# A mixture-of-experts kernel: the routers' token-valued tile table written by VectorE token by token

## The reference, cut to what matters

```python
logits = flat @ router_w.T
probs = softmax(logits)
topk_prob, topk_idx = top_k(probs, 2)
topk_prob = topk_prob / sum(topk_prob)
for e in range(8):
    w_e = sum(topk_prob * (topk_idx == e))
    y = (silu(flat @ gate_w[e].T) * (flat @ up_w[e].T)) @ down_w[e].T
    out = out + w_e * y
```

## Time and profile before

| | |
|---|---|
| median of 3 runs | 1080.37 us (1078.08 to 1084.45) |
| profiled execution | 1077.55 us, its span 1075.7 us |
| TensorE busy | 917.6 us of the span |
| VectorE busy | 609.9 us |
| ScalarE busy | 551.9 us |
| first tail, line 527's first start to line 541's start | 120.27 to 138.84 us |
| second tail, the same | 810.12 to 828.67 us |
| mean granted TensorE clock | 0.898 |

### The profile page before, as it was taken

How to read it: one execution, slowest core, us unless ns; L and a number is a source line. 1 busy time by engine, 2 the same in 40 slices (tenths; PEclk the granted TensorE clock), 3 DMA queues, 4 the chain that set the end, 5 groups by cost and what they waited for, 6 DMA issues and landing times. The chain is left out here.

```text
span 1075.7 us, 20700 instructions
## 1 busy us (share of the span) xinstructions
PE 917.6 (85%) x6102; PEld 785.6 (73%) x6102; DVE 609.9 (57%) x1702; ACT 551.9 (51%) x1372; POOL 271.2 (25%) x274
## 2 busy tenths in 40 slices
PE   5656569999999999997378999998746899998998
PEld 3544458888888888886256777776625899997998
DVE  6887942332323323222777778767768555555786
ACT  6346543443434434343355555554436566667774
POOL 0000031121211212110763220000001544443775
PEclk9858569999999999999589999998655899999999
DMA  9655211111111111111843221102241344444654
GB/s 385 271 193 198 81 40 55 54 55 54 50 54 55 55 54 50 55 44 66 270 128 98 60 79 60 40 21 79 79 157 42 116 138 139 137 133 131 182 163 148
DMA packets 62231, 114.79 MB, mean 107 GB/s; under 512 B 9586, under 2 KB 43012, under 8 KB 60996
## 3 DMA queue, kind: packets, MB, share of 16 engines
q1 hardware_dynamic: 48900, 77.77, 20.5%
q0 software_dynamic: 12960, 35.41, 11.6%
q10 hardware_dynamic: 288, 0.47, 0.1%
HBM read 74.01 MB, written 39.59 MB: 106 GB/s over the span
## 5 line engine op out<-in xcount | busy, mean ns | idle before, releaser
L600 POOL DMA_INDIRECT experts_rows_sb<-h_rows,choices x142 | 137.5, 969 | 651.9 <-POOLq L428 325.9
L799 DVE TENSOR_TENSOR experts_a_sb<-experts_a_sb,experts_bankU 128x512 f32<-128x512 f32 x71 | 48.9, 689 | 223.1 <-PE experts_bankU L184 223.1
L747 ACT ACTIVATE experts_a_sb<-experts_bankG 128x512 f32<-128x512 f32 (+1 forms) x142 | 69.7, 491 | 90.4 <-PE experts_bankG L184 90.3
L760 ACT ACTIVATE experts_y_sb<-experts_bankY 128x256 f32<-128x256 f32 x142 | 54.7, 385 | 86.1 <-PE experts_bankY L181 66.6
L738 ACT ACTIVATE experts_hT<-experts_bankH 128x256 fp32r<-128x256 f32 x142 | 54.2, 382 | 80.5 <-PE experts_bankH L663 80.4
L1198 POOL DMA_INDIRECT attn_y<-y_rows,choices x64 | 65.6, 1024 | 108.3 <-DVE x_res L1652 55.9
L182 PE MATMUL experts_bankY<-down_high,experts_aT 128*128 x284 | 91.5, 322 | 0.3 <-DVE experts_aT L187 0.3
L183 PE MATMUL experts_bankY<-down_low,experts_aT 128*128 x284 | 79.8, 281 | 0.0
L184 PE MATMUL experts_bankY<-down_high,experts_aT 128*128 x284 | 79.8, 281 | 0.0
L923 POOL DMA_INDIRECT shared_y<-y_rows,choices x64 | 67.9, 1061 | 37.8 <-POOLq L555 18.5
L181 PE MATMUL experts_bankY<-down_plain,experts_aT_plain 128*128 x284 | 72.9, 379 | 0.0
(11 more groups left out here) (367 smaller groups left out, 2626.4 us busy)
## 6 DMA issues: line engine op xcount, KB each, us to landing
y_rows<-experts_y_sb SPq DMA_DIRECT2D x142, 128.0 KB, 1.9
h_rows<-xn SPq DMA_DIRECT2D x32, 256.0 KB, 2.2
mix_xT<-in_xt SPq DMA_DIRECT2D x4, 1024.0 KB, 12.0
x_res<-in_x SPq DMA_DIRECT2D x4, 1024.0 KB, 13.9
gate_raw<-in_L_ffn_gate_w SPq DMA_DIRECT2D x2, 2048.0 KB, 13.6
up_raw<-in_L_ffn_up_w SPq DMA_DIRECT2D x1, 4096.0 KB, 25.1
x_rows<-x_res SPq DMA_DIRECT2D x16, 256.0 KB
x_res<-x_rows SPq DMA_DIRECT2D x8, 512.0 KB, 4.7
```

Of the source, the lines that this page charges most:

```text
L600: nc.gpsimd.indirect_dma_start(rows[t % DEPTH][:, :], None, h_dram, bass.IndirectOffsetOnAxis(ap=ids_i[:, t:t + 1], axis=0)).then_inc(s_ro ...
L747: nc.scalar.activation(a_sb[i % RING][:, :], bankG[i % RING][:, 0:hidden], ACT.Silu if gate is not None else ACT.Relu).then_inc(s["act"], 1)
L799: nc.vector.tensor_tensor(a_sb[i % RING][:, :], a_sb[i % RING][:, :], bankU[i % RING][:, 0:hidden], ALU.mult).then_inc(s["a"], 1)
```

## The change

The tile table is written by VectorE with four instructions of 128x72 per batch, one for each tile of tokens. Each has two scalars per partition from memory: it compares the ramp with the token's `slot_tile` (`is_equal`) and multiplies the result by the token's number (`mult`). ScalarE's multiplication and the semaphore between VectorE and ScalarE are left out; the row table's instruction now signals `one_hot` itself. Both tails use the function, so both change.

```diff
-                s_equal, s_one_hot, s_spread = ([sem(f"{tag}_{n}{k}") for k in range(2)] for n in ("equal", "one_hot", "spread"))
+                s_one_hot, s_spread = ([sem(f"{tag}_{n}{k}") for k in range(2)] for n in ("one_hot", "spread"))
...
                     nc.scalar.activation(share[:, :], apart[:, :], ACT.Exp).then_inc(s["exp"], 1)
-                    for n in range(TILES // BATCH):
-                        for k in range(2):
-                            act.wait_ge(s_equal[k], n + 1)
-                            for i in range(BATCH):
-                                part = at_tile[k][n % RING][:, i * TABLE_T:(i + 1) * TABLE_T]
-                                last = nc.scalar.activation(part, part.bitcast(F32), ACT.Copy, scale=token[:, n * BATCH + i:n * BATCH + i + 1])
-                            last.then_inc(s_one_hot[k], 1)
...
                             if n >= RING:
                                 dve.wait_ge(s_spread[k], n - RING + 1)
-                            nc.vector.tensor_tensor(table(at_tile[k][n % RING]), K("ramp")[:, 0:TABLE_T].unsqueeze(1).broadcast_to([P, BATCH, TABLE_T]),
-                                                    tokens(slot_tile, at_j, TABLE_T), ALU.is_equal)
+                            for i in range(BATCH):
+                                nc.vector.tensor_scalar(at_tile[k][n % RING][:, i * TABLE_T:(i + 1) * TABLE_T], K("ramp")[:, 0:TABLE_T],
+                                                        slot_tile[:, at_j + i:at_j + i + 1], token[:, n * BATCH + i:n * BATCH + i + 1],
+                                                        ALU.is_equal, ALU.mult)
                             nc.vector.tensor_tensor(table(at_row[k][n % RING]), K("ramp").unsqueeze(1).broadcast_to([P, BATCH, P]),
-                                                    tokens(slot_row, at_j, P), ALU.is_equal).then_inc(s_equal[k], 1)
+                                                    tokens(slot_row, at_j, P), ALU.is_equal).then_inc(s_one_hot[k], 1)
```

## The result

The changed kernel takes 1092.7 us (median of 4 runs, 1091.91 to 1093.48), the kernel before 1079.22 (median of 4, 1077.1 to 1084.45). The ratio is 1.0111, with a 95% interval of 1.0084 to 1.0137, which is 9.1 to 14.8 us of 1079.22. So it is slower, by 13.5 us between the medians; the forecast's step from before to after, 15.2 us, lies 0.4 us above the upper end of that interval. The profiled execution took 1092.98 us (span 1091.1), 15.43 more than the profiled one of before.

The account below looks back on a forecast made before the run. The router tails lie on the path, VectorE and ScalarE level there. Per tail, 16 x (0.93 - 0.37) = 9.0 us less 1.30 gives 7.6 within rounding; two add 15.2 to 1080.37: 1095.6, likeliest 1095.5, range 1087 to 1106.

Parts of the forecast that it names:

- The bound: Both router tails: nothing of the expert stage runs beside them, so a change in their length shifts all behind.
- The spacing of the new instruction: VectorE's 128x72 instruction with two scalars from memory: 0.232 us from start to start, 0.93 for four.
- ScalarE's lag: End of each tail: ScalarE's last scaling ends after VectorE's last comparison; removing the scalings saves 1.30 us a tail.
- The small chain: VectorE's 1.40 us of work behind the batches: stays hidden by about 0.3 us under the 1.65 until the ids' read.
- The sum: A tail of 64 spacings plus 11.33 us: 26.2 us, 7.6 more than 18.57; two tails +15.2.
- The time: Whole kernel: likeliest 1095.5 us, from the median before of 1080.37 and the two tails' added time.
- The clock: TensorE's granted clock: 0.50 in the tails; its later rise may move by 3 us, 1.5 us a tail, range only.
- TensorE's wait between batches: In the tails, TensorE waits for VectorE about 0.65 us between batches.
- A: Rival: scalars read beside the instruction before, spacing 0.11 us, a tail of 18.4 us, kernel 1080.0; chance 0.10.
- B: Rival: new instruction starts when the last ends, spacing 0.316 us, kernel 1106.4; chance 0.15 together with spacing unshrunk by size.

Follow-up runs that it names:

- e4: The change in the second tail only, the first tail as in the kernel before: 1085.63 us, ratio 1.0059 to the kernel before.
- e1: The changed kernel with two constants in place of both scalars from memory in the four 128x72 instructions: 1081.97 us.
- e2: The kernel before with the tile table compared by four 128x72 instructions with one scalar from memory, ScalarE's scaling kept: 1086.72 us.
- e3: The changed kernel with each of the four small instructions 128 columns wide instead of 72: 1097.9 us.
- e6: The kernel before with both tables in float16 and their operands laid out in pairs, ScalarE scaling as before: 1078.0 us.
- e9: The changed kernel with float16 tables and the row table's operands in pairs: 1083.82 us.

## Why the prediction was right

- *The bound.* Right: the tails' length lies on the path, and all that follows shifts by it. From the read of the ids to TensorE's restart it is 7.29 us before and 7.28 after, and e4's tails add.
- *The spacing of the new instruction.* 0.232 forecast, 0.228 measured; the duration 0.316 and 0.311. It came from a row of another size with the same operands, corrected by a slope from rows with constants. e1, e2 and e3 show each term: 0.07 for the instruction, 0.06 per scalar from memory, 0.5 ns per element. The forecast batch was 1.53, measured 1.51.
- *ScalarE's lag.* Right: 1.30 us go from the end, and from the last row comparison's end (144.23) to the read (145.88) it is 1.65 us, as assumed. The small chain (lines 528 to 534 now) ends at 145.56 and stays hidden.
- *The sum.* 26.2 us a tail forecast, 25.9 measured; +15.2 forecast, +14.7 in the tails, +15.43 between the two profiled executions, +13.5 between the medians, with an interval of 9.1 to 14.8 that leaves out the 15.2 and holds the 14.7. So the tails' step was forecast 0.5 us too large, mostly by the spacing (64 x 0.004 us a tail).
- *The time.* 1095.5 forecast, 1092.7 measured. 1.2 of the 2.8 us are the base: one more run moved the median of before from 1080.37 to 1079.22. The rest is the 0.5 of the two tails and scatter outside them, which the runs don't divide.
- *The clock.* As expected, 0.50 in the tail. The rise came some 0.5 us later behind TensorE's restart, well inside the 3 us allowed for, and e4 shows that it moves by as much without the change.
- *A small miss.* TensorE's wait between batches is 0.45 us, not 0.65. I had counted from start to start of its matmuls, and the profile counts a group's time to the end of the last one (1.07 us).
- *The rivals.* A is what e1 shows (18.18 us a tail), and it fails on the scalars. The table in the Trainium skill (VectorE: DVE Perf Modes, "The TRN2 errata — SBUF-src ops pay a fixed extra latency per instruction") makes an estimate of (58 + 36)/0.96 = 98 ns for a 128x72 instruction; with constants the trace shows a spacing of 108, with two scalars from memory 228. So the table is 10 ns below the first, and has no term for the second. B needed a spacing as long as the duration; in the changed kernel it is 0.08 us shorter (0.228 against 0.311), and in the other kernels 0.08 to 0.10. The sentence of the Trainium skill that the prediction sets beside B (VectorE: DVE Perf Modes, "The DRAIN you can't avoid") has an exception in the same paragraph, which the prediction left out: "A next op that is not held starts earlier". So the section does not ask for B of instructions that are not held, and the overlaps in these traces do not contradict it.

## What to carry to other kernels

Before work is moved to an engine to save a hop, compare the engines' times per batch: here the freed one (ScalarE, 0.99 us a batch) worked beside the loaded one (VectorE, 0.97), so all that could be won was the lag of one batch at the end, 1.30 us, and every addition to VectorE counted sixteen times. A `tensor_scalar` with scalars from memory is not the cheap fusion that it looks like when it is short: 0.06 us each, before any element, so one large instruction with repeated operands beats four short ones with two such scalars. The spacing from start to start is what adds up; take it from a row with the same kind of operands, and correct the size by a slope.

## What the hardware showed beyond that

In float16, the speed of `tensor_tensor` depended on the layout of its operands alone: 0.60 us for 128x512 with stride zero innermost in the repeated one, 0.34 with each value stored twice and an innermost run of two in all. And with float16 tables, a group of four 128x72 matmuls took 0.42 us (e6, e9) in place of the 1.07 in the changed kernel, both at a granted clock of 0.50, the 1.2 GHz level.
